# Fp32 one-hot blocks made a chunk ahead, keys by a broadcast DMA, and ScalarE's node work in another order, in a graph network on one core

## The reference

```python
x = _layernorm(x + _L0_gnn_ref(...))  # tanh(segment_sum(sigmoid(att) * x[tail]) @ W)
x = _layernorm(x + _L1_gnn_ref(...))  # 5 GAT layers, one head
x = _layernorm(x + _L2_gnn_ref(...))  # one dot-product attention layer
x = _layernorm(x + _L3_gnn_ref(...))  # 3 layers, 4 heads, with edge features
```

```python
h = x @ W
al = h @ a_src
ar = h @ a_dst
logit = jax.nn.leaky_relu(al[src] + ar[dst], SLOPE)
alpha = _segment_softmax(logit, dst, n)
out = jax.ops.segment_sum(alpha[:, None] * h[src], dst, num_segments=n)
return out + b
```

## Time and profile before

| | us |
|---|---|
| median of 3 runs | 11675.39 (11665.48 to 11681.93) |
| profiled execution | 11682.55 |
| its span | 11680.8 |
| POOL busy | 8705.9 (75%) |
| DVE busy | 6969.9 (60%) |
| PE busy | 4520.9 (39%) |
| ACT busy | 3033.7 (26%) |

### The profile page before, as it was taken

One profiled execution on the slowest core, in us unless ns is written; L12 is line 12 of the kernel. 1 busy time (PEld: TensorE's weight loads), 2 busy tenths in 40 slices (PEclk: granted clock), 3 DMA queues, 4 the chain that ended last, 5 costly groups with the idle time before them and its releaser, 6 DMA issues. The chain is left out here.

```text
span 11680.8 us, 81322 instructions
## 1 busy us (share of the span) xinstructions
PE 4520.9 (39%) x21281; PEld 2989.0 (26%) x21281; DVE 6969.9 (60%) x10721; ACT 3033.7 (26%) x3657; POOL 8705.9 (75%) x8304
## 2 busy tenths in 40 slices
PE   5433335653663665466366400001111422242222
PEld 5433322322332332233233200001111322232222
DVE  6333336664664665466466545554555688858887
ACT  1010112112112111211211222222332354534543
POOL 7888877777776776777677677767776777767775
PEclk7555557876886787688588755555555555555555
DMA  5333332221221222122233333333333444434442
GB/s 180 36 36 33 33 60 53 57 60 40 59 60 41 57 60 54 43 60 57 51 104 102 89 105 114 114 95 102 116 117 103 126 144 145 146 103 144 144 146 88
DMA packets 569608, 1015.35 MB, mean 87 GB/s; under 512 B 305748, under 2 KB 370232, under 8 KB 558280
## 3 DMA queue, kind: packets, MB, share of 16 engines
q0 software_dynamic: 378304, 398.64, 18.3%
q1 hardware_dynamic: 139398, 305.47, 7.8%
q10 hardware_dynamic: 51842, 310.55, 6.8%
HBM read 596.88 MB, written 430.03 MB: 88 GB/s over the span
## 5 line engine op out<-in xcount | busy, mean ns | idle before, releaser
L818 POOL DMA_INDIRECT turned<-d_t,idx x6516 | 6436.2, 988 | 1993.6 <-issue 1993.6
L930 PE MATMUL banks<-wide 128*128 128x462 bf16 x11340 | 2521.9, 388 | 1530.8 <-DVE wide L1055 1530.8
L930 PEld LDWEIGHTS banks<-wide 128*128 128x128 bf16 x11340 | 1166.2, 104 | 2852.2 <-DVE wide L1055 1406.1
L1077 DVE COPY idx<-src 128x28 int32 x252 | 45.6, 181 | 2398.1 <-DMA turned<-d_t,idx 2322.8
L627 POOL DMA_INDIRECT d_acc<-work,idx x784 | 1240.5, 1582 | 251.0 <-issue 235.4
L961 PE MATMUL banks<-ident,wide 128*128 128x128 f32 x994 | 283.8, 434 | 2652.1 <-ACT wide L838 1269.1
L887 ACT ACTIVATE banks<-factors 128x28 f32<-128x28 f32 (+1 forms) x252 | 55.7, 221 | 4120.2 <-DVE factors L1143 4120.2
L1170 DVE TENSOR_TENSOR_SCAN wide<-banks,wide 128x224 f32<-128x224 f32 (+1 forms) x1008 | 1024.1, 1078 | 5.8
L961 PEld LDWEIGHTS banks<-ident,wide 128*128 128x128 f32 x994 | 188.3, 230 | 2724.9 <-ACT wide L838 1325.9
L1154 DVE TENSOR_TENSOR wide<-turned,banks 128x1792 f32<-128x1792 f32 x252 | 872.1, 3461 | 0.0
L1049 DVE TENSOR_TENSOR_SCAN wide<-banks,wide 128x448 f32<-128x448 f32 (+1 forms) x725 | 658.1, 910 | 174.1 <-ACT banks L842 166.5
(11 more groups left out here) (300 smaller groups left out, 8327.7 us busy)
## 6 DMA issues: line engine op xcount, KB each, us to landing
d_e<-wide ACTq DMA_DIRECT2D x168, 924.0 KB
turned<-d_t,idx POOLq DMA_INDIRECT x6516
d_e<-wide ACTq DMA_DIRECT2D x84, 1008.0 KB
wide<-d_b SPq DMA_DIRECT2D x60, 1344.0 KB
wide<-d_b SPq DMA_DIRECT2D x60, 896.0 KB, 4.6
wide<-d_edge SPq DMA_DIRECT2D x86, 448.0 KB, 7.2
d_b<-wide SPq DMA_DIRECT2D x28, 1344.0 KB, 5.0
d_b<-zeros ACTq DMA_DIRECT2D x1, 25088.0 KB, 75.7
```

Of the source, the lines that this page charges most:

```text
L818: gp.indirect_dma_start(rows[:, b, k, :], None, table[:, :], offset(idx[:, b, k:k + 1])).then_inc(s["gathered"][b], 16)
L930: mm = nc.tensor.matmul(ps_col[:, i, :], hot[:, i, j, :], flat(split[:, part, j * SET:(j + 1) * SET, :]), start=j == 0 and part == 0, stop ...
```

## The change

In `prepare` the keys are turned once for all chunks by PE and stored to DRAM in the order of chunks (`d_key`). In `edges` SP loads a chunk's keys to all partitions by a broadcast DMA into one of two buffers, DVE compares them with the first rows, kept in PSUM, and writes fp32 blocks, of which there are two sets; the set for chunk c + 3 is made at the end of chunk c, counted with 1 for the first. PE multiplies the fp32 block with `g.proj` itself, one matmul a set, 28 a chunk, into four banks that are waited for and given back one by one. The split into three parts, and its sums in PSUM over 21 matmuls, are gone. In `nodes` ACT does the work for the next group (`before_projection`: tanh, the copy of the rows turned for `mix`, and `functions`) between the copy of the rows turned for `project` and the copy of the product.

```diff
@@ def prepare
+        sp.wait_ge(s["keys_set"], 2)
+        sp.dma_start(g.d_key.rearrange("(r p) -> r p", p=P), turned_keys[:]).then_inc(s["keys_stored"], 16)
+        sp.wait_ge(s["keys_stored"], 16)
...
+        v.wait_ge(s["keys_turned"], 1)
+        nc.vector.tensor_copy(turned_keys[:], ps_turn).then_inc(s["keys_set"], 1)
...
+        pe.wait_ge(s["keys_set"], 1)
+        nc.tensor.transpose(ps_turn, flat(set_row[:]), g.ident[:]).then_inc(s["keys_turned"], 1)
@@ def edges
+    def chunk_keys(n):
+        return g.d_key[bass.ds(n * X * P, X * P)].partition_broadcast(P)
...
+            if X and more:
+                sp.sem_inc(s["sp_steps"], 1)
+                sp.wait_ge(s["hot_made"], X * (chunk + 1))
+                sp.dma_start(keys[:, 1 - b], chunk_keys(chunk + 3)).then_inc(s["keys_loaded"][1 - b], 16)
...
-            for c0, c1 in GROUPS:
-                nc.scalar.copy(split[:, 0, c0:c1, :], g.proj[:, c0:c1, 0:TW]).then_inc(s["split_hi"], 1)
...
-            for i in range(X):
-                pe.wait_ge(s["hot_made"], X * (n - 1) + i + 2)
+            for i in range(X):
+                if not first:
+                    pe.wait_ge(s["cols_taken"], X * (n - 2) + i + 1)
+                pe.wait_ge(s["hot_made"], X * (n - 1) + i + 1)
                 for j in range(SETS):
-                    for part in range(3):
-                        mm = nc.tensor.matmul(ps_col[:, i, :], hot[:, i, j, :],
-                                              flat(split[:, part, j * SET:(j + 1) * SET, :]),
-                                              start=j == 0 and part == 0, stop=j == SETS - 1 and part == 2)
+                    mm = nc.tensor.matmul(ps_cols[i], hot[:, place, i, j, :],
+                                          flat(g.proj[:, j * SET:(j + 1) * SET, :]),
+                                          start=j == 0, stop=j == SETS - 1)
...
+            nc.vector.tensor_copy(ps_first, first_rows).then_inc(s["first_copied"], 1)
...
-                nc.vector.tensor_tensor(hot[:, i], mid(ps_key[:, i, :], SETS), bc(first_rows, P),
+                nc.vector.tensor_tensor(hot[:, place, i], mid(keys[:, place, i, :], SETS), bc(ps_first, P),
                                         ALU.is_equal).then_inc(s["hot_made"], 1)
...
-                v.wait_ge(s["cols_done"], X * (chunk + 1))
-                link(nc.vector.tensor_tensor(found[:], ps_col.rearrange("p x (c w) -> p x c w", w=TW), bc(member[:], TW),
-                                             ALU.mult))
+                for i in range(X):
+                    v.wait_ge(s["cols_done"], X * chunk + i + 1)
+                    nc.vector.tensor_tensor(found[:, i], ps_cols[i].rearrange("p (c w) -> p c w", w=TW),
+                                            bc(member[:, i], TW), ALU.mult).then_inc(s["cols_taken"], 1)
...
-                one_hots(chunk + 2)
+                one_hots(1 - b, t + 2)
@@ def nodes, ACT
+        def before_projection(j):
             if summing:
...
             if mix and j + 1 < NG:
                 copy_turned("mix", j + 1)
             functions(j)
+
+        if mix:
+            copy_turned("mix", 0)
+        before_projection(0)
+        for j in range(NG):
             if out_w:
                 copy_turned("project", j)
...
+            if j + 1 < NG:
+                before_projection(j + 1)
+            for k, (k0, k1) in enumerate(pieces if out_w else ()):
+                act.wait_ge(s["multiplied"], NB * j + k + 1)
+                nc.scalar.copy(out[:, j * GC + k0:j * GC + k1, 0:out_w],
```

More of the change, by code:

```diff
@@ L657, in edge_tiles @@
     if X:
-        tiles.update(hot=[P, X, SETS, P // 2], split=[P, 3, C, TW // 2], found=[P, X, SET, TW])
+        tiles.update(hot=[P, 2, X, SETS, P], keys=[P, 2, X, P], found=[P, X, SET, TW])
     return dict(rows=[P, 2, K, TW]), tiles
@@ L737, in edges @@
     if X:
-        key_f = ph.sbuf("key_f", [P, X])
         member = ph.sbuf("member", [P, X, SET])
-        hot, split, found = tiles["hot"].bitcast(BF16), tiles["split"].bitcast(BF16), tiles["found"]
+        hot, keys, found = tiles["hot"], tiles["keys"], tiles["found"]
         first_rows = g.row.rearrange("p (s c) -> p s c", c=SET)[:, :, 0]
-        rest = flat(tiles["state"].rearrange("p b k r -> p (b k) r"))[:, 0:C * TW].rearrange("p (c w) -> p c w", w=TW)
-        ps_key = banks[:, 0, 0:X * P].rearrange("p (x e) -> p x e", e=P)
-        ps_col = banks[:, 1:1 + X, 0:SET * TW]
+        ps_first = banks[:, 0, 0:SETS]
+        ps_cols = [banks[:, 1 + i, 0:SET * TW] for i in range(X)]
     ps_eT, ps_em, ps_we, ps_same, ps_w, ps_keep = (
@@ L775, in _ @@
                 sp.dma_start(gs[:], a["e_norm"].partition_broadcast(P)).then_inc(s["loaded"], 16)
+        for n in range(1, 3 if X else 1):
+            sp.dma_start(keys[:, n % 2], chunk_keys(n)).then_inc(s["keys_loaded"][n % 2], 16)
         if clear is not None:
@@ L782, in _, with one @@
             sp.dma_start(b_rows[:], edge_rows(spread)[:, c * K:c * K + K, :]).then_inc(s["b_loaded"], 16)
[L783 to L800, removed]
+        def one(t, b, more):
+            chunk = 2 * t + b
+            cols = bass.ds(chunk * K, K)
+            if multi:
+                if update:
+                    sp.wait_ge(s["e_stored"][b], 16 * (t + 1))
+                sp.sem_inc(s["sp_steps"], 1)
+                sp.dma_start(e_rows[:, b], edge_rows(g.d_edge)[:, cols, :]).then_inc(s["e_loaded"][b], 16)
+            sp.wait_ge(s["b_turned"], chunk + 2)
+            sp.dma_start(b_rows[:], edge_rows_after(spread, 2 * K)[:, cols, :]).then_inc(s["b_loaded"], 16)
+            if X and more:
+                sp.sem_inc(s["sp_steps"], 1)
+                sp.wait_ge(s["hot_made"], X * (chunk + 1))
+                sp.dma_start(keys[:, 1 - b], chunk_keys(chunk + 3)).then_inc(s["keys_loaded"][1 - b], 16)
+            if clear is not None:
+                sp.dma_start(edge_rows(clear)[:, cols, :], zeros[:]).then_inc(s["e_stored"][b], 16)
+            if kind == "dot":
+                sp.dma_start(edge_rows(g.d_edge)[:, cols, :],
+                             edge_rows(a["edge_pad"])[:, cols, :]).then_inc(s["e_stored"][b], 16)
+        pairs(sp, one)
         if kind == "dot" or clear is not None:
@@ L1471, in copy_turned @@
                                ps_turn[i][0:w, 0:(k1 - k0) * P]).then_inc(s["turn_copied"], 1)
-        if mix:
-            copy_turned("mix", 0)
-        for j in range(NG):
+        def before_projection(j):
             if summing:
```

74 lines of the change are left out of this document (27 added, 47 removed).

## The result

The changed kernel takes 11651.81 us (median of 13 runs, 11639.98 to 11656.34), the kernel before in the same session 11677.76 (13 runs, 11665.48 to 11684.69): ratio 0.9975, 95% interval 0.9968 to 0.9982. That is 26 us by the medians and 29 by the ratio; 30.8 were forecast.

A forecast was written before the change was run, and what follows sets the result against it. POOL's issuing was taken as the bound. Gains of 7.7 (split), 10.9 (first node stage) and 12.2 us (node stage before the dot layer) sum to 30.8, giving 11644.6 us; range 11627 to 11668.

The forecast's parts named there:

- The bound: Edge loops: POOL's gathers wait for nobody; 24 of 1.25 us make a GAT chunk of 29.96 us.
- fp32 blocks, 0: GAT chunks: PE's 56 fp32 instructions take 24.2 us, clock raised after 5 us, hidden under 30 us; cost 0.
- the cover's edge: GAT chunks: beyond some 29.4 us of PE a chunk, each further us costs 1 us times 135 sets.
- Rival 1: GAT chunks: fp32 clock stays at 1.2 GHz, a set takes 43.1 us, PE bounds; 1700 us more, 13350 us; 5%.
- DVE's part and the key loads, 0: GAT chunks: DVE ends some 0.1 us later out of 9.28 us of slack, keys load a chunk ahead; cost 0.
- The split: Before GAT edge loops: its removal ends lengthened POOL issues, saving 7.7 us in four stages, 1.75 in the first.
- In all other node stages the order gives nothing: Other node stages: POOL has no wait for ACT but three of 0.3 us, so ACT's new order gains nothing.
- First node stage: First node stage: ACT's new order and the absent split bring the seed 10.9 us sooner, bounds 7 to 13.
- Node stage before the dot layer: There: group period falls from 17.05 to 11.8 us and POOL's waits go, saving 12.2 us (11 to 13).
- Everything behind it, 0: Dot edge stage and first edge stage of kind multi: the forecast sum has no term for them.
- Rival 3: Node stages: ACT's new order gives half, 19 us gained in all, 11657 us; 17%.
- Rival 4: Split's delay returns by key loads or the first two one-hot calls; only the orders count: 23 us, 11652; 8%.

The follow-up runs named there:

- e6: Changed kernel with PE multiplying the first two of four picked columns twice, 84 instructions a chunk in place of 56: 11916.96 us, ratio 1.0216.
- e7: Changed kernel with five picked columns in place of four, so 23 gathered columns a chunk on POOL and 70 PE instructions: 11466.83 us, ratio 0.9831.
- e5: Changed kernel with the four one-hot operations reading the sets' first rows from SBUF, not PSUM: 11828.67 us, ratio 1.0139.
- e3: Changed kernel with ACT's node work back in the old order, so fp32 blocks and no split alone: 11666.89 us, ratio 0.9997.
- e2: Kernel before with the new order of ACT's node work alone, three bf16 parts and split kept: 11640.74 us, ratio 0.9974.
- e11: Kernel before, with DVE waiting for its index copy before the first product in the dot and first multi edge stages: 11639.90 us, ratio 0.9978.
- e12: Kernel before again, no edit, for a second profile: 11664.77 us, ratio 0.9999.
- e9: Changed kernel with one extra unused DVE reduction before the first product in the dot and first multi edge stages: 11627.60 us, ratio 0.9967.
- e8: Changed kernel with five picked columns and DVE's wait for its index copy in the dot and first multi edge stages: 11437.90 us, ratio 0.9804.
- e10: Changed kernel with two extra unused DVE reductions before the first product in the dot and first multi edge stages: 11657.11 us, ratio 0.9992.
- e1: Changed kernel again, no edit, for a second profile: 11644.92 us, ratio 0.9975.
- e4: Changed kernel, with DVE waiting for its index copy before the first product in the dot and first multi edge stages: 11611.72 us, ratio 0.9948.

## Why the prediction was right, step by step

- **The bound.** Right: POOL issuing. GAT edge stages 866.4 and 866.5 us.
- **fp32 blocks, 0.** Right, with 24.2 us a set as forecast, and the clock raised 5 us in. e6 and e7 stand on the two sides of the cover's edge: at 27.4 us of PE in a chunk of 28.7 it is free, at 32.5 PE sets the chunk's length. Rival 1 (the clock stays down) is out. What the text didn't see is that a PE which nearly bounds doesn't pay the half-clock start at all.
- **DVE's part and the key loads, 0.** Right: 9.0 us of slack for 9.28. e5 shows that this hangs on one operand; the rule as the prediction put it (two SBUF inputs hold POOL up, one in PSUM doesn't) is now measured on the disputed operation itself.
- **The split, -7.7 in four stages and -1.75 in the first.** Right in the main: e3 has -1.7 each, 6.6 in four, and -1.8. In the first two profiles these four stages gave 10.3, since the order changed them too, and since executions of the same code differ there (135.15 us a stage in the kernel before's first profile, 134.11 in e11's and e12's). "In all other node stages the order gives nothing" was wrong by 0.8 us a stage, as e2 has it. It had looked for waits only. POOL doesn't wait there, but the order moves DVE's normalising, whose products with two SBUF inputs lengthen POOL's issues.
- **First node stage, -10.9.** It gave 13.3, counted from layer 0's end. The first spread came 3.0 later (3.7 forecast) and groups 10.75 apart (10.9 to 11.05). The mis-sized term is POOL's own 10.54 us a group: that was taken over from before, with issues of 2.36 and 1.25 us in it; now it is 10.75 less 1.45 of wait plus 0.30, 9.6.
- **Node stage before the dot layer, -12.2.** 11.8, and the waits went as said.
- **Everything behind it, 0.** Wrong by 10.5 us in this pair of profiles, and by about 9 on average. This is the term that was missing, a cost from the change in two stages whose instructions it leaves as they are.

So the sum, 30.8, against 26 to 29 measured, is good to 5 us from two errors of opposite sign: 5 us more from the node stages, 9 to 10 lost to collisions. The mechanism of each gain was right; that the total came so near is in part luck. Rival 3 (the order gives half) is out by e2. Rival 4 named the time that was measured, 11652, with a gain of 23 us, for a wrong reason: the split's delay didn't come back by key loads or one-hot calls.

## What to carry to other kernels

When POOL's indirect DMAs are the bound, list the DVE operations with two SBUF inputs that run beside them and put one operand in PSUM, if it is small; here 7 columns decide over some 180 us. Where that can't be done, look at the phase: products 1.86 us apart kept step with issues that they had lengthened to 1.56 + 0.30, and one wait of 0.1 us ahead of them gave 33 us in the changed kernel and 25 in the kernel before, about as much as the whole change. And when a change hides an engine's work, look what the slack buys: a fifth column on PE was worth six times the rest.

## What the runs showed of the hardware that was not expected

- In these rows the hold works one way. POOL's issue loses up to 0.76 us to one of DVE's products of 0.94, and a product that starts in the middle of an issue takes 0.93 to 1.01 us, as do those that start between two issues. The Trainium skill, SBUF — State Buffer, SBUF: two separate sides, calls the pair an exclusive lock for which the other side fully blocks; for POOL the rows agree, for DVE none shows it.
- A blocked issue ends 0.83 us behind the DVE operation, nearly its whole length of 0.945. So it loses what it waits, less 0.11 us at most, however long it waited.
- Bare issues in the GAT stages took 0.946 us on average in the first profiles of both kernels and in e9's, 0.944 in e2, e3, e5, e6, e7, e8, e10, e11 and e12's, and 0.945 in e1's and e4's. Over a GAT edge stage that is some 1.6 us, and over the kernel some 15 us, as much as many a change, in executions of the same code. Spans of single profiles are compared stage by stage for this reason.
- PE's clock after an idle gap: behind 4.8 us of idle time or more, the 135 sets of the changed kernel have 0.50 over their first us, but for three with 0.53 to 0.59; behind 1.6 us or less, e7's sets start at 1.00.
